# Twelve edge projections made at the head of the node layers, and another order of tiles in ball attention

## The reference, cut to what matters

```python
xn = _layernorm(x, axis=-1)
x = x + gnn_attention(xn, src, dst) + linear_attention(xn)
x = x + ffn_mixture(_layernorm(x))                 # 8 experts, all of them for every node
xn = _layernorm(x, axis=-1)
# second graph layer
e = edge_attr_384 @ W_edge.T + b_edge              # 50,000 x 384 x 256
h = xn @ W_node.T + b_node
agg = segment_sum(e * h[src], dst)
x = x + silu(agg) @ base_w.T + spline_bases(agg) @ spline_w
# ball attention, of the same xn
h = relu(batchnorm(logmap0(proj(xn)) @ w_qkv))     # 768 channels
...                                                # grouped products, out @ w_res + b_res
x = x + ball_attention(xn)
x = x + expert_of_highest_probability(x)
```

## Time and profile before

| | us |
|---|---|
| timed runs (3) | 2994.89, 2996.53, 3007.01; median 2996.53 |
| profiled execution, its own time | 3003.98 |
| its span, first to last instruction | 3002.3 |
| attention sums, node layers | 684 to 918, 921 to 1557 |
| edge convolution | 1558 to 2172 |
| spline layer, ball attention | 2180 to 2448, 2449 to 2640 |

### The profile page before, as it was taken

One profiled execution on the slowest core, in us unless ns is written; L12 is line 12 of the kernel. 1 busy time (PEld: TensorE's weight loads), 2 busy tenths in 40 slices (PEclk: granted clock), 3 DMA queues, 4 the chain that ended last, 5 costly groups with the idle time before them and its releaser, 6 DMA issues. The chain is left out here.

```text
span 3002.3 us, 55005 instructions
## 1 busy us (share of the span) xinstructions
PE 2628.1 (88%) x11924; PEld 2063.7 (69%) x11925; DVE 2118.2 (71%) x4277; ACT 1398.0 (47%) x2962; POOL 1054.9 (35%) x1184
## 2 busy tenths in 40 slices
PE   7777787778994999999989999999889968879698
PEld 6545564465552777777758888888768856657587
DVE  6686678878888765665337888888899959955411
ACT  3323332228882343443324444444389948845122
POOL 1576777732110000000016666666400008800043
PEclk9997899999996999999989999999989989989799
DMA  4798999937774000000037777777501140042353
GB/s 160 242 310 266 296 311 307 321 87 227 228 225 140 31 1 9 9 1 9 16 109 209 213 215 213 216 212 216 161 27 40 40 153 34 1 179 90 103 172 127
DMA packets 236865, 444.84 MB, mean 148 GB/s; under 512 B 29041, under 2 KB 128817, under 8 KB 235340
## 3 DMA queue, kind: packets, MB, share of 16 engines
q1 hardware_dynamic: 179790, 262.93, 27.9%
q0 software_dynamic: 56960, 180.47, 19.1%
HBM read 351.60 MB, written 92.69 MB: 148 GB/s over the span
## 5 line engine op out<-in xcount | busy, mean ns | idle before, releaser
L1911 PE MATMUL bank<-sums 128*128 128x256 f32 x2352 | 543.1, 381 | 2.6 <-issue 2.6
L1987 POOL DMA_INDIRECT conv_h<-table_h,conv_ix x392 | 374.5, 955 | 289.0 <-ACT conv_ix L1958 168.0
L1911 PEld LDWEIGHTS bank<-sums 128*128 128x128 f32 x2352 | 435.1, 191 | 55.2 <-issue 3.0
L1714 ACT ACTIVATE area<-bank,nodes_bi,nodes_sc 128x320 f32<-128x320 f32 x320 | 197.5, 617 | 332.1 <-PE bank L1634 332.1
L725 POOL DMA_INDIRECT x<-table_qv,scores_ix x300 | 283.8, 946 | 183.4 <-ACT scores_ix L626 104.5
L1884 DVE SCALAR_TENSOR_TENSOR x<-bank,nodes_w,x 128x256 f32<-128x256 f32 x200 | 96.4, 484 | 216.1 <-PE bank L1643 215.9
L1447 PE MATMUL bank<-attend_pv,x 128*128 128x260 f32 x800 | 220.5, 404 | 26.8 <-POOL attend_pv L1377 24.6
L745 PE MATMUL bank<-sums,area 128*128 x800 | 228.1, 413 | 11.1 <-issue 6.2
L1447 PEld LDWEIGHTS bank<-attend_pv,x 128*128 128x128 f32 x800 | 137.6, 191 | 109.5 <-issue 62.8
L2008 DVE TENSOR_TENSOR conv_msg<-bank,conv_h 128x512 f32<-128x512 f32 x196 | 135.6, 692 | 102.9 <-PE bank L1911 93.3
L1958 ACT ACTIVATE conv_ix<-src 128x2 int32 x196 | 39.9, 203 | 360.5 <-DVE conv_msg L2008 347.4
(11 more groups left out here) (486 smaller groups left out, 5806.1 us busy)
## 6 DMA issues: line engine op xcount, KB each, us to landing
sums<-in_edges SPq DMA_DIRECT2D x196, 384.0 KB, 3.4
x<-edge_v SPq DMA_DIRECT2D x200, 256.0 KB, 3.0
edge_v<-x SPq DMA_DIRECT2D x150, 256.0 KB, 4.9
hidden_rows<-top_wide SPq DMA_DIRECT2D x25, 512.0 KB, 3.4
projected<-spline_hst SPq DMA_DIRECT2D x10, 960.0 KB, 4.4
ball_hT<-projected SPq DMA_DIRECT2D x5, 1920.0 KB, 19.4
top_wd<-in_top_wd SPq DMA_DIRECT2D x8, 1024.0 KB, 14.2
x<-in_x SPq DMA_DIRECT2D x10, 640.0 KB, 9.5
```

What stands on the lines that cost most here:

```text
L1714: nc.scalar.activation((h1, h2)[layer][:, o, hf * CW:(hf + 1) * CW], banks[n % HIDS][:, 0:CW], ACT.Relu, scale=sc[:, layer, e, o:o + 1], b ...
L1911: mm = nc.tensor.matmul(banks[u][:, g * F:(g + 1) * F], m.conv_eT[:, u, g, c], m.conv_w[:, c], start=False, stop=c == EC - 1, skip_group_c ...
L1987: nc.gpsimd.indirect_dma_start(out=h[:, u, g, :], out_offset=None, in_=m.d_h, in_offset=bass.IndirectOffsetOnAxis(ap=ix[:, u * G + g:u * G ...
```

## The change

1. **Node layers.** Before the rounds PE opens five banks with bf16 zeros and projects the attributes of eleven steps (`project_ahead`), and of a twelfth after the first turn. They are the last step of every second round of the convolution: 7, 15, ... 95. SP loads the edge bias and weight and the attributes of each (384 KB) ahead of or between the other loads (a ring of six in the room of the weights of experts 1 to 3). ACT seeds the banks and copies results out (a ring of five in the room of `h1` and `h2`, two apart for the last two), and SP stores them to DRAM (`d_ahead`, 256 KB each). ACT's copies stand in its program between the small operations of round -1 (`kept_before`). The loads of the other chunks of x, of the weights of experts 1 to 7 and of the experts' output biases come behind all of the stores. The scales of the experts are made later in round -1.
2. **Edge convolution.** The loops of SP, ACT, DVE and PE run twelve times over two rounds and then over single rounds. In the second round of each pair the last step isn't projected and its bank isn't seeded; SP loads its stored projection into the slot of its attributes, DVE's message reads it there, and SP refills that slot only after that message.
3. **Spline and ball.** The last two units of columns (tiles 20 to 24) stay in `m.rows` (`m.last_hT`) and aren't stored. Ball attention takes tile 20 to 24 first, then 0 to 19; only those are loaded back. The scales wait for the norms' load alone; relu goes tile by tile for the first two; the rest of the first chunk is split, three channel tiles on ACT and three on DVE (`rectify`, two instructions each); `wres` is loaded behind the first chunk of h.

```diff
+AHEAD_STEPS = 12
+                sp.dma_start(ahead_b, a["gnn1_bedge"]).then_inc(ahead_b_in, 16)
+                sp.dma_start(ahead_w, a["gnn1_wedge"]).then_inc(ahead_w_in, 16)
+                for j in range(3):
+                    edges_ahead(j)
                 for to, x in ((raw[:, 0], "ffn_bn1"), (raw[:, 1], "ffn_bn2")):
                     sp.dma_start(to, a[x]).then_inc(bn_loaded, 16)
                 sp.dma_start(m.x[:, tiles(0)], a["x"][0:CH].rearrange("(t p) f -> p t f", p=P)).then_inc(x_back[0], 16)
+                for j in range(3, IN_RING):
+                    edges_ahead(j)
...
+                for j in range(IN_RING, AHEAD_STEPS):
+                    edges_ahead(j)
+                    store_ahead(j - IN_RING)
+                    if j == IN_RING + 1:
+                        for k, x in enumerate(("ffn_w1", "ffn_w2", "ffn_wo")):
+                            sp.dma_start(W[0][:, k], a[x][0]).then_inc(wload[0], 16)
+                for j in range(AHEAD_STEPS - IN_RING, AHEAD_STEPS):
+                    store_ahead(j)
...
                     if e == 0:
+                        sp.wait_ge(ahead_made, AHEAD_STEPS)
                         sp.dma_start(near_bo[:], a["ffn_bo_near"]).then_inc(bo_loaded, 16)
...
+                def project_ahead(j):
+                    pe.wait_ge(ahead_in[j % IN_RING], 16 * (j // IN_RING + 1))
+                    pe.wait_ge(ahead_seeded, j + 1)
+                    bank = ahead_bank(j)
+                    for g in range(G):
+                        for k in range(EC):
+                            mm = nc.tensor.matmul(bank[:, g * F:(g + 1) * F], ahead_eT[:, j % IN_RING, g, k], ahead_w[:, k], start=False,
+                                                  stop=k == EC - 1, skip_group_check=True)
+                    mm.then_inc(ahead_made, 1)
+                for u in range(AHEAD_BANKS):
+                    mm = nc.tensor.matmul(banks[u][:, 0:G * F], m.zeros[:].bitcast(BF16)[:, 0:P], m.zeros[:].bitcast(BF16)[:, 0:G * F],
+                                          start=True, stop=True)
+                mm.then_inc(ahead_opened, 1)
+                pe.wait_ge(ahead_w_in, 16)
+                for j in range(AHEAD_STEPS - 1):
+                    project_ahead(j)
...
+                kept_before = {2: (0, 3), 4: (3, 8), 6: (8, AHEAD_STEPS - 1), 7: (AHEAD_STEPS - 1, AHEAD_STEPS)}
...
+                        if c < 0 and e in kept_before:
+                            keep_ahead(*kept_before[e])
...
# edge convolution, SP
+                with sp.Fori(0, AHEAD_STEPS) as r:
+                    for u in range(UN - 1):
+                        edges_in(r * 2 + 1, u)
+                    sp.wait_ge(messaged, r * (2 * UN) + 2 * UN)
+                    sp.sem_inc(free, 1)
+                    sp.dma_start(m.conv_made, m.d_ahead[:, bass.ds(r, 1)].rearrange("p o g f -> p (o g) f")).then_inc(arrived[UN - 1], 16)
                     for u in range(UN):
+                        edges_in(r * 2 + 2, u)
...
# DVE
-                    nc.vector.tensor_tensor(msg[:, u % 2], wide(u), h[:, u], ALU.mult).then_inc(messaged, 1)
+                    nc.vector.tensor_tensor(msg[:, u % 2], m.conv_made if ahead else wide(u), h[:, u], ALU.mult).then_inc(messaged, 1)
...
# PE
+                def round_of(r, after, ahead):
                     for u in range(UN):
-                        if u + 2 < UN:
+                        if u + 2 >= UN:
+                            project(after, u + 2 - UN)
+                        elif not ahead:
                             project(r, u + 2)
-                        else:
-                            project(r + 1, u + 2 - UN)
+                        elif u + 2 < UN - 1:
+                            project(r, u + 2, 2)
                         add_up(r, u)
+                with pe.Fori(0, AHEAD_STEPS) as r:
+                    round_of(r * 2, r * 2 + 1, False)
+                    round_of(r * 2 + 1, r * 2 + 2, True)
+                with pe.Fori(2 * AHEAD_STEPS, last) as r:
+                    round_of(r, r + 1, False)
...
# ball attention
-                for k in range(MT):
-                    relu(0, k, 0, 2 * P)
+                for t in range(2):
+                    for k in range(MT):
+                        relu(0, k, t * P, (t + 1) * P)
                 length(0)
                 scale(0)
+                for k in range(REST):
+                    relu(0, k, 2 * P, CH)
                 length(1)
-                for k in range(MT):
-                    relu(0, k, 2 * P, CH)
```

More of the change, by code:

```diff
@@ L1853, in _ @@
                                     dve.wait_ge(h_stored, 16 * q)
+                                else:
+                                    for u in range(2):
+                                        dve.wait_ge(ahead_stored[OUT_RING + u], 16)
                                 if q == TU - 1:
@@ L1971, in _ @@
                 last = last_round(act, m)
-                with act.Fori(0, last) as r:
+                with act.Fori(0, AHEAD_STEPS) as r:
+                    for u in range(UN):
+                        sources(r * 2 + 1, u)
+                        round_off(r * 2, u)
+                        if u < UN - 1:
+                            seed(u, 2 if u == UN - 2 else 1)
+                    for u in range(UN):
+                        sources(r * 2 + 2, u)
+                        round_off(r * 2 + 1, u)
+                        seed(u)
+                with act.Fori(2 * AHEAD_STEPS, last) as r:
                     for u in range(UN):
@@ L2028, in _ @@
                 rest(0, 0)
-                with dve.Fori(0, last) as r:
+                def round_of(r, after, ahead):
                     for u in range(UN):
-                        message(r if u + 2 < UN else r + 1, (u + 2) % UN)
-                        rest(r if u + 1 < UN else r + 1, (u + 1) % UN)
+                        message(r if u + 2 < UN else after, (u + 2) % UN, ahead=ahead and u + 2 == UN - 1)
+                        rest(r if u + 1 < UN else after, (u + 1) % UN)
                         keep(r, u)
+                with dve.Fori(0, AHEAD_STEPS) as r:
+                    round_of(r * 2, r * 2 + 1, False)
+                    round_of(r * 2 + 1, r * 2 + 2, True)
+                with dve.Fori(2 * AHEAD_STEPS, last) as r:
+                    round_of(r, r + 1, False)
                 for u in range(UN):
@@ L2107, in _ @@
             def _(sp):
-                for n in range(NC):
+                for n in range(NC - 2):
                     sp.wait_ge(h_kept, MT * (n + 1))
@@ L2440, in _ @@
                 dve.sem_inc(widened, 1)
+                for k in range(REST, MT):
+                    rectify(k)
                 def reach(t):
```

208 lines of the change are left out of this document (154 added, 54 removed).

## The result

The changed kernel takes 2972.57 us (median of four runs, 2967.08 to 2973.94), the kernel before 3000.70 beside it (2994.89 to 3007.01): the ratio is 0.9898, with a 95% interval of 0.9883 to 0.9913. The forecast was 2969.5 in a range of 2956 to 2986, and faster. The profiled execution after took 2973.42, its span is 2971.7; against the profiled one before that is 30.6 us less, where the sum of the terms said 27.0.

A forecast was written before the change was run, and what follows sets the result against it. PE was taken to bound the convolution and DVE ball attention; 13.3 + 2.2 + 11.5 = 27.0 us off the profiled 3003.98 gave 2977.0, less 7.45 to the median 2969.5. Range 2956 to 2986.

The forecast's parts named there:

- What paces what: PE sets the convolution's pace, 3.06 us a step against DVE's 2.60; DVE paces the node layers' head and ball attention.
- the rival in which PE loses nothing: Convolution: DVE has stored up slack, so 29.9 us gained in place of 13.3, 2953 us in all; chance 0.08.
- the one in which VectorE paces all: Convolution: VectorE paces it and the twelve projections are hidden anyway, 0 gained there, 2983 us; chance 0.12.
- The term 12 x 1.11 = 13.3: Convolution: of each missing projection's 2.49 us PE waits 1.38 and keeps 1.11, over twelve steps 13.3 us.
- by the rows the message begins at T + 0.62: Convolution: T starts the sum ahead of the missing projection; DVE's message begins 0.62 later, its remainder ends at T + 1.91.
- the doubled bodies for their branch: Convolution: taken as 0; the rival has a stall at each pass's branch, 41 us (3010) or 82 (3051), chance 0.04.
- Nothing late behind a skip: Convolution: DVE is last by 0.4 us for one step, then PE again; the slot's refill is covered by 2.6 us.
- Head, 2.2: Node layers' head: turn stays at 957, PE comes warm, logits at 963.1 instead of 965.33, 2.2 us gained.
- The rival of a head that stays cold: Node layers' head: PE stays at 1.2 GHz between projections, 26 us lost where 2.2 gained was counted, 2998; chance 0.08.
- "isn't seen": Node layers' head: DVE's chain moves by 2.2 us; what the sixteen matmuls of 6.78 us save beyond that doesn't show.
- Ball attention, 11.5: Ball attention's start: second reciprocal 11.1 us earlier, third 11.5, from there DVE's loop; 11.5 us gained, ends 9.4 and 13.2.
- Spline stage 0: Spline stage: the two stores not made and other waits taken away ended before their stage did, 0 us gained.

The follow-up runs named there:

- a skip where the 0.62 holds: Changed kernel with a skip in every four steps, 24 in all, the added ones reading another step's stored rows (wrong sums): 2959.73 us, ratio 0.9854.
- with zeros: Changed kernel with matmuls of zeros on TensorE in its waits at the start of ball attention (12, 12 and 10): 2966.74 us, ratio 0.9874.
- zeros that overrun the wait: Changed kernel with 18 matmuls of zeros on TensorE behind the second output tile of the first expert: 2975.74 us, ratio 0.9906.
- an order that only moves it: Changed kernel with the first expert's outputs added on VectorE ahead of the second folding of the edge sums: 2977.57 us, ratio 0.9900.
- 7.3 us of f32 zeros: Changed kernel with its five banks opened by f32 zeros instead of bf16 zeros at the head of the node layers: 2977.83 us, ratio 0.9895.

## Why the prediction was right, point by point

- **What paces what: right.** PE gained only what VectorE's remainder leaves it, the rival in which PE loses nothing (29.9 us) and the one in which VectorE paces all (0) both fell with the idling of PE at a skip, 0.99 us between its matmuls, and the kernels with no, six and twelve skips lie on one line.
- **The term 12 x 1.11 = 13.3 was mis-sized; it measured 12 x 1.336 = 16.0.** The main step that failed is "by the rows the message begins at T + 0.62". That is the row of the same step in the loop before; in the doubled body it begins at T + 0.41, and the remainder ends 0.21 sooner. Two smaller ones nearly cancel: PE goes on 0.12 behind the remainder's end and not 0.04, and the sum behind the wait is 0.10 shorter, which the sum didn't have. 1.11 + 0.21 - 0.08 + 0.10 = 1.34. At a skip where the 0.62 holds, 1.13 was measured. I had costed the doubled bodies for their branch and not for when the message begins. That doubling alone moves that step's message by 0.2 us is shown by the kernel in which nothing is skipped; that the register operation is what makes the 0.2 us is argued, from the fact that both go together.
- **Nothing late behind a skip: right.** VectorE is last for one step (1705.46), the ahead message never waits for its load, and there is no wait for the refilled slot.
- **Head, 2.2: near, for partly wrong reasons.** The turn was forecast at 957 and came at 958.3, the first expert at 963 and came at 964.1, in a stage that begins 0.6 later. The rival of a head that stays cold fell: PE's granted clock was 0.50 for the first 6 us of the projections and 1.00 behind them. Over the traces the first output comes 2.4 to 3.1 us earlier after the stage's start than with the old head (55.8 to 56.4, against 58.8 to 58.9; 57.6 in the profile after). From the stage's start to the first message of the convolution it takes 646.6 to 650.2 us in the three traces with the old head and 643.6 to 647.0 in eight with the new one: some 3 us by the medians, with an overlap. That PE's gain beyond VectorE's "isn't seen" held; that PE then stands 4.4 to 4.7 us and pays for it in clock was missing, and some of the saving went there.
- **Ball attention, 11.5: it measured 11.1** at the second reciprocal, as forecast, 11.2 at the third, where 11.5 was forecast, and 10.7 from the fourth on. The first length came 9.1 earlier after the stage's start (9.4 said). Some 0.35 of the missing part is the cold fourth `widen`: that step of VectorE takes 6.64 us and not 6.29, and with zeros 6.14. The next takes 6.79 with and without zeros, for one VectorE instruction of 1.20 us where 0.69 was the rule; the forecast took 6.29 for it. All this is against one trace of the old order; two others have the second reciprocal at 37.8 and 39.1 and not 36.4, where the new order without zeros has 25.2 to 25.9 in nine, so the gain lies between 10.5 and 13.9 by the pair that is taken.
- **Spline stage 0: the profile shows 3.4**, of the clock, not of the stores. From the last reciprocal to the end 2.1 went back. What the forecast did not have (3.4 in the spline stage, 1.1 in the first steps of the convolution, less 2.1 and 0.6) comes to 1.8 of the 3.6 us by which 30.6 exceeds 27.0; the rest is the 2.7 of the twelve skips less 1.0 at the head and in ball attention.
- **From profile to median.** The 7.45 us between them were more than the runs bear out: beside the changed kernel the median before was 3000.70, later 3004 to 3008. The changed kernel's own profile is 0.85 over its median. So the forecast of 2969.5 took off 6.6 us too many there and missed 3.6 in the terms, which leaves it 3.1 under the 2972.57: that it lies so near is partly luck.

## What to carry to other kernels

Moving work from a stretch that one engine paces into a stretch where it stands idle pays by what the next chain leaves, not by what is moved: here 1.34 of 2.49 us. Price it from the start times at that very step of the new loop body, doubled and with nothing moved yet, not from the same step of the old one. And where a wait of PE is filled, as at the start of ball attention, its next matmuls come at full clock: ball attention ends 2.2 us sooner, while zeros that overrun the wait, and an order that only moves it, gain nothing or lose.

## What the runs showed of the hardware that I had not expected

- The granted clock of PE after an idle stretch came back at a different moment in nearly identical streams: ten microseconds of the spline stage held 35 matmuls at 0.73 or 48 at 1.00, 3 us for the stage. The first output of the node layers came 57.6 or 56.4 us after the stage's start in two traces of the same kernel.
- 2.3 us of bf16 zeros and 3.4 us of idling ahead of the projections left them slow (granted clock 0.50 in their first 3 us, 30.5 us in all); 7.3 us of f32 zeros and 0.85 us of idling left them fast (1.00, 28.7 us). The zeros' length and the idling weren't varied apart.
- Whether a wait is followed by a register operation of 53 ns or by a plain one of 21 ns goes with 0.2 us at the instruction behind it. Writing a loop body out twice changed this in one step of eight.
